# Second weight buffers and an earlier place for the ternary work in the first feed-forward layer of an adaLN transformer block

## The reference

```python
h = _layernorm(x, axis=-1) * (1 + ca) + sa
x = x + ga * _L0_attn_ref(h, wq, wk, wv, wo)
h = _layernorm(x, axis=-1) * (1 + cb) + sb
x = x + gb * _L0_ffn_ref(h, w1, w2, w3)
...
def activation_quant(x):
    scale = 127.0 / jnp.clip(jnp.max(jnp.abs(x), axis=-1, keepdims=True), EPS, None)
    return jnp.clip(jnp.round(x * scale), -128, 127) / scale
def weight_quant(w):
    scale = 1.0 / jnp.clip(jnp.mean(jnp.abs(w)), EPS, None)
    return jnp.clip(jnp.round(w * scale), -1, 1) / scale
def bitlinear(x, w):
    xn = rmsnorm(x)
    xq = xn + jax.lax.stop_gradient(activation_quant(xn) - xn)
    wq = w + jax.lax.stop_gradient(weight_quant(w) - w)
    return jnp.einsum('bsi,oi->bso', xq, wq)
h = jax.nn.silu(bitlinear(x, w1)) * bitlinear(x, w2)
return bitlinear(h, w3)
```

## Time and profile before

| what | us |
|---|---|
| median of 2 runs | 9290.5 (9260.4 to 9320.6) |
| the profiled execution | 9303.3 |
| its span on core 3, the slowest | 9301.7 |
| spans of the 8 cores | 9230.1 to 9301.7 |
| TensorE matmuls busy | 3531.4 (38%) |
| VectorE busy | 3765.0 (40%) |
| ScalarE busy | 1250.3 (13%) |
| GpSimd busy | 51.4 (1%) |

### The profile page before, as it was taken

How to read it: one execution, slowest core, us unless ns; L and a number is a source line. 1 busy time by engine, 2 the same in 40 slices (tenths; PEclk the granted TensorE clock), 3 DMA queues, 4 the chain that set the end, 5 groups by cost and what they waited for, 6 DMA issues and landing times.

```text
span 9301.7 us, 51813 instructions; the slowest of 8 cores (9230.1 to 9301.7 us)
## 1 busy us (share of the span) xinstructions
PE 3531.4 (38%) x12512; PEld 1341.4 (14%) x12512; DVE 3765.0 (40%) x5792; ACT 1250.3 (13%) x1963; POOL 51.4 (1%) x100
## 2 busy tenths in 40 slices
PE   2436666666744002344434434321111111115555
PEld 0112222222311001111111111110000000002111
DVE  3241122222213784222222222247777777762222
ACT  0135555353311000000000000000000000000000
POOL 0000000000000000000000000000000000000000
PEclk8666667677766556677677677665555555558777
DMA  9615555353033000111111111110000000014433
GB/s 156 112 27 149 154 158 145 107 150 78 19 89 77 23 0 31 61 61 52 61 61 52 61 61 52 61 41 24 24 24 24 24 27 24 24 43 121 121 120 122
DMA packets 391015, 655.95 MB, mean 71 GB/s; under 512 B 44547, under 2 KB 192006, under 8 KB 386560
## 3 DMA queue, kind: packets, MB, share of 16 engines
q1 hardware_dynamic: 376896, 560.35, 19.6%
q0 software_dynamic: 13824, 92.28, 5.8%
HBM read 693.97 MB, written 50.51 MB: 80 GB/s over the span
## 4 chain that ended last, share of the span: by engine, by line
DVE 37%; PE 23%; DMA 17%; issue 10%; ACT 6%; SPq 5%; DVEq 1%; ACTq 0%; POOLq 0%
DMA wfl<-w 11%; DVE sm L1282 8%; PE ps L1125 6%; DVE tmpb L1279 5%; PE ps L1136 5%; PE ps L1346 3%; PE ps L613 3%; DMA mring<-wmod 2%; DVE sm L1068 2%; PE ps L640 2%; PE ps L850 2%; DVE ternB L1120 2%; DVE ternA L1114 2%; ACT esb L753 1%; DVEq L74 1%
## 5 line engine op out<-in xcount | busy, mean ns | idle before, releaser
L1346 PE MATMUL ps<-q3c,ternA 128*128 128x512 bf16 x2048 | 729.9, 528 | 2354.3 <-DVE ternA L1324 2353.9
L1125 PE MATMUL ps<-q,ternA 128*128 128x512 bf16 x2048 | 572.3, 449 | 1563.5 <-DVE ternB L1120 1563.5
L1282 DVE TENSOR_TENSOR sm<-sm,tmpb 128x512 f32<-128x512 f32 x1024 | 708.8, 692 | 109.9 <-DVE tmpb L1279 4.1
L1346 PEld LDWEIGHTS ps<-q3c,ternA 128*128 128x128 bf16 x2048 | 242.0, 124 | 2842.2 <-issue 2775.1
L1149 DVE TENSOR_TENSOR rbc<-ps,du1b 128x512 f32<-128x512 f32 x128 | 88.5, 692 | 1061.0 <-PE ps L1136 1054.0
L1125 PEld LDWEIGHTS ps<-q,ternA 128*128 128x128 bf16 x2048 | 223.8, 112 | 1912.9 <-issue 1754.5
L1279 DVE TENSOR_SCALAR tmpb<-sm 128x512 f32<-128x512 f32 x1024 | 437.5, 427 | 111.0 <-DVE sm L1282 2.7
L1136 PE MATMUL ps<-q,ternB 128*128 128x512 bf16 x2048 | 452.5, 379 | 0.0
L1318 DVE TENSOR_SCALAR terntmp<-wfl,wsc 128x512 f32<-128x512 f32 x256 | 124.5, 486 | 802.6 <-DMA wfl<-w 802.5
L1363 ACT ACTIVATE kraw<-ps,modv 128x512 f32<-128x512 f32 x32 | 22.0, 687 | 3053.0 <-PE ps L1346 2965.7
L742 PE MATMUL ps<-qsb,ksb 128*128 128x512 bf16 x512 | 274.8, 549 | 335.6 <-ACT esb L753 249.9
(11 more groups left out here) (201 smaller groups left out, 4129.8 us busy)
## 6 DMA issues: line engine op xcount, KB each, us to landing
wfl<-w SPq DMA_DIRECT2D x1024, 256.0 KB, 4.4
rbc<-w SPq DMA_DIRECT2D x256, 256.0 KB, 3.9
wfl<-w SPq DMA_DIRECT2D x512, 128.0 KB, 2.3
mring<-wmod POOLq DMA_DIRECT2D x24, 2048.0 KB, 18.0
q3c<-q3s SPq DMA_DIRECT2D x384, 128.0 KB, 2.2
xst<-x2s SPq DMA_DIRECT2D x32, 512.0 KB, 3.7
hs<-hch SPq DMA_DIRECT2D x128, 128.0 KB, 1.7
hch<-hs SPq DMA_DIRECT2D x128, 128.0 KB, 2.2
```

Of the source, the lines that this page charges most:

```text
L1125: st("tensor", lambda e, th=th, kc=kc: e.matmul((psA if th == 0 else psB)[:, 0:512], ternA[:, kc * 128:(kc + 1) * 128], q12[:, kc * OWN + ...
L1282: st("vector", lambda e, tb=tb, bb=bb: e.tensor_tensor(out=tb, in0=tb, in1=bb, op=ALU.subtract))
L1346: tsl=tsl: e.matmul(psx[:, 0:512], tsl[:, di * 128:(di + 1) * 128], qsl[:, th * 512:(th + 1) * 512], start=(k3 == 0), stop=(k3 == NFC - 1)),
```

## The change

The loop body's loads and ternary work become two functions, `f1_loads` and `f1_tern`. Both are called for chunk 0 ahead of the loop, and in turn `dc2` for chunk `dc2 + 1`, ahead of the matmuls and the evacuation of chunk `dc2`. Odd chunks get buffers of their own: `wfl3` and `wfl4` for the weights, `ternA2` and `ternB2` for their ternary form. The first of the four ternary instructions now waits for the matmuls two chunks back instead of one. The first product of odd chunks goes to psE and psF, and its first matmul waits for L1149's successor of two chunks back (`w_hv[("udq", ...)]`). psC and psD, `terntmp`, `hch`, `rbc`, `sm2` and `sqb2` stay single or as they were.

```diff
--- before.py
+++ after.py
@@ -150,6 +150,10 @@
     cq3b = K.sb("cq3b", [128, 1024], F32, KB(89))
     do3b = K.sb("do3b", [128, 1024], F32, KB(93))
     terntmp = K.sb("terntmp", [128, 2048], F32, KB(97))
+    ternA2 = K.sb("ternA2", [128, 2048], BF16, KB(143))
+    ternB2 = K.sb("ternB2", [128, 2048], BF16, KB(147))
+    wfl3 = K.sb("wfl3", [128, 2048], F32, KB(159))
+    wfl4 = K.sb("wfl4", [128, 2048], F32, KB(167))
     ternA = K.sb("ternA", [128, 2048], BF16, KB(105))
     ternB = K.sb("ternB", [128, 2048], BF16, KB(109))
     hch = K.sb("hch", [128, 2048], BF16, KB(113))
@@ -1088,10 +1092,10 @@
     w_hv = {}
     w_maxi3 = st("vector", lambda e: e.memset(maxac[:, :], 0.0),
                  waits=[(sVE, w_q12)] + ([(sDBG5, 32)] if "d_cqb" in DBG else []))
-    for dc2 in range(NFC):
+    def f1_loads(dc2):
         sW = sW0 if dc2 % 2 == 0 else sW1
-        w_dst1 = wfl if dc2 % 2 == 0 else wfl2
-        w_dst2 = wfl2 if dc2 % 2 == 0 else wfl
+        w_dst1 = wfl if dc2 % 2 == 0 else wfl3
+        w_dst2 = wfl2 if dc2 % 2 == 0 else wfl4
         for cc in range(4):
             st("sync", lambda e, dc2=dc2, cc=cc, w_dst1=w_dst1: e.dma_start(
                 out=w_dst1[:, cc * 512:(cc + 1) * 512],
@@ -1102,47 +1106,64 @@
                 out=w_dst2[:, cc * 512:(cc + 1) * 512],
                 in_=w2_d[dc2][:, 4 * cc:4 * cc + 4, :]),
                inc=sW, inck=16)
-        w_wld = sW.n
-        wslc1 = wfl if dc2 % 2 == 0 else wfl2
-        wslc2 = wfl2 if dc2 % 2 == 0 else wfl
+        return sW.n
+
+    def f1_tern(dc2, w_wld):
+        sW = sW0 if dc2 % 2 == 0 else sW1
+        wslc1 = wfl if dc2 % 2 == 0 else wfl3
+        wslc2 = wfl2 if dc2 % 2 == 0 else wfl4
+        tA = ternA if dc2 % 2 == 0 else ternA2
+        tB = ternB if dc2 % 2 == 0 else ternB2
         st("vector", lambda e, wslc1=wslc1: e.tensor_scalar(
             out=terntmp[:, :], in0=wslc1[:, :], scalar1=wsc[:, 0:1], scalar2=-1.0,
             op0=ALU.is_ge, op1=ALU.add),
            waits=[(sW, w_wld), (sVE, w_negt)] +
-                 ([(sMM, w_f1mm.get(dc2 - 1, 0))] if dc2 >= 1 else
+                 ([(sMM, w_f1mm.get(dc2 - 2, 0))] if dc2 >= 2 else
                   [(sDBG2, sDBG2.n)]))
-        st("vector", lambda e, wslc1=wslc1: e.scalar_tensor_tensor(
-            out=ternA[:, :], in0=wslc1[:, :], scalar=wsc[:, 6:7], in1=terntmp[:, :],
+        st("vector", lambda e, wslc1=wslc1, tA=tA: e.scalar_tensor_tensor(
+            out=tA[:, :], in0=wslc1[:, :], scalar=wsc[:, 6:7], in1=terntmp[:, :],
             op0=ALU.is_gt, op1=ALU.add))
         st("vector", lambda e, wslc2=wslc2: e.tensor_scalar(
             out=terntmp[:, :], in0=wslc2[:, :], scalar1=wsc[:, 1:2], scalar2=-1.0,
             op0=ALU.is_ge, op1=ALU.add))
-        w_tern[dc2] = st("vector", lambda e, wslc2=wslc2: e.scalar_tensor_tensor(
-            out=ternB[:, :], in0=wslc2[:, :], scalar=wsc[:, 7:8], in1=terntmp[:, :],
+        w_tern[dc2] = st("vector", lambda e, wslc2=wslc2, tB=tB: e.scalar_tensor_tensor(
+            out=tB[:, :], in0=wslc2[:, :], scalar=wsc[:, 7:8], in1=terntmp[:, :],
             op0=ALU.is_gt, op1=ALU.add))
+
+    w_ld = {0: f1_loads(0)}
+    f1_tern(0, w_ld[0])
+    for dc2 in range(NFC):
+        if dc2 + 1 < NFC:
+            w_ld[dc2 + 1] = f1_loads(dc2 + 1)
+            f1_tern(dc2 + 1, w_ld[dc2 + 1])
+        tA = ternA if dc2 % 2 == 0 else ternA2
+        tB = ternB if dc2 % 2 == 0 else ternB2
+        psU0 = psA if dc2 % 2 == 0 else psE
+        psU1 = psB if dc2 % 2 == 0 else psF
         for th in range(2):
             for kc in range(NKC):
-                st("tensor", lambda e, th=th, kc=kc: e.matmul(
-                    (psA if th == 0 else psB)[:, 0:512],
-                    ternA[:, kc * 128:(kc + 1) * 128],
-                    q12[:, kc * OWN + th * 512: kc * OWN + (th + 1) * 512],
-                    start=(kc == 0), stop=(kc == NKC - 1)),
+                st("tensor", lambda e, th=th, kc=kc, tA=tA, psU0=psU0, psU1=psU1:
+                   e.matmul(
+                       (psU0 if th == 0 else psU1)[:, 0:512],
+                       tA[:, kc * 128:(kc + 1) * 128],
+                       q12[:, kc * OWN + th * 512: kc * OWN + (th + 1) * 512],
+                       start=(kc == 0), stop=(kc == NKC - 1)),
                    waits=([(sVE, w_tern[dc2]), (sVE, w_q12)] +
-                          ([(sVE, w_hv.get((dc2 - 1, th), 0))])
+                          ([(sVE, w_hv.get(("udq", dc2 - 2, th), 0))])
                           if kc == 0 else []),
                    inc=(sMM if kc == NKC - 1 else None))
         for th in range(2):
             for kc in range(NKC):
-                st("tensor", lambda e, th=th, kc=kc: e.matmul(
+                st("tensor", lambda e, th=th, kc=kc, tB=tB: e.matmul(
                     (psC if th == 0 else psD)[:, 0:512],
-                    ternB[:, kc * 128:(kc + 1) * 128],
+                    tB[:, kc * 128:(kc + 1) * 128],
                     q12[:, kc * OWN + th * 512: kc * OWN + (th + 1) * 512],
                     start=(kc == 0), stop=(kc == NKC - 1)),
                    waits=([(sVE, w_hv.get((dc2 - 1, th), 0))] if kc == 0 else []),
                    inc=(sMM if kc == NKC - 1 else None))
         w_f1mm[dc2] = sMM.n
         for th in range(2):
-            psu = psA if th == 0 else psB
+            psu = psU0 if th == 0 else psU1
             pst2 = psC if th == 0 else psD
             hsl = hch[:, ((2 * dc2 + th) % 4) * 512:(((2 * dc2 + th) % 4) + 1) * 512]
             sHSp = sHS[(2 * dc2 + th) % 4]
@@ -1152,6 +1173,7 @@
                waits=[(sMM, w_f1mm[dc2])] +
                      ([(sHSp, sHSp.n)] if dc2 >= 2 else []))
             w_udq = sVE.n
+            w_hv[("udq", dc2, th)] = w_udq
             st("scalar", lambda e, th=th: e.activation(
                 out=sm2[:, th * 512:(th + 1) * 512], in_=rbc[:, th * 512:(th + 1) * 512],
                 func=AF.Silu), waits=[(sVE, w_udq)])
```

## The result

The changed kernel takes 8294.5 us (median of 11 runs, 8251.9 to 8345.5) against 9277.1 us before (median of 10 runs, 9260.4 to 9331.9): 0.893 of the time, 95% interval 0.890 to 0.896. The prediction was 8285 us, range 8235 to 8430. The profiled execution took 8321.8 us.

A forecast was written before the change was run, and what follows sets the result against it. Load, ternary work, matmuls and evacuation in the first feed-forward layer stood in line, 41.07 us a turn; overlapped, 24.9 us. Over 63 turns that saves 1019 us from 9303.3, forecasting 8285 us, range 8235 to 8430.

The forecast's parts named there:

- The ring before: First feed-forward layer: load, ternary work, matmuls and evacuation follow one another without overlap, 40.95 us against 41.07 measured a turn.
- VectorE's branch: First feed-forward layer, before evacuation: load 10.38, ternary work 7.59, next instruction 0.10, together 18.07 us.
- TensorE's branch: Beside VectorE's work: last sum-of-squares matmul 1.62, about 0.1, then 16.10 us of matmuls, together 17.8 us before evacuation.
- The 0.3 us for the later of two near branches: Added to the 24.58 us turn because the later branch varies from turn to turn, giving 24.9 us.
- The added wait ahead of the evacuation: On VectorE's queue, evacuation stands behind instructions waiting for a load, so the load's 10.38 us stay on the path.
- E: As a moment: the second `hch` product's end. As a rival: work stays in line with matmuls, near 9300 us, chance 0.01.
- Clock: each turn starts slow as before: TensorE's pause shrinks to 8.2 us, still long enough for its clock to fall; the 16.10 us of matmuls stay.
- Rival A: Reduced clock, 0.81, on die 0 in the first feed-forward layer: turn 27.1 us, time 8423 us, chance 0.12.
- B: Rival: TensorE's clock stays at 1.2 GHz, matmuls 28.3 us, turn 36.5 us, time 9015 us, chance 0.04.
- C: Rival: loads land later, meeting other cores' loads; at 2 us more, turn 26.6 us, time 8391 us, chance 0.08.
- D: Rival: slower, late loads block VectorE's queue; with a 30 us load, turn 44.2 us, time 9500 us, chance 0.01.
- The sum: First feed-forward layer: 63 turns save 16.17 us each, 1019 us, other stages unchanged; 8285 us.

The follow-up runs named there:

- e1: The changed kernel with the next chunk's ternary work put back behind the evacuation, its load still early: 8802.1 us, 0.944 of before.
- e6: The changed kernel with one VectorE instruction of the ternary work doubled: 8458.9 us, 0.908 of before.
- e4: The changed kernel with the sum-of-squares matmuls behind the next chunk's first 32 matmuls, plus a second sqb buffer: 8319.9 us, 0.891 of before.
- e3: The changed kernel with loads issued two chunks ahead, same buffers: 8217.9 us, 0.881 of before.
- e5: The changed kernel with both loads two chunks ahead and sum-of-squares matmuls behind the next chunk's first 32: 7757.5 us, 0.832 of before.
- e2: The changed kernel without the second PSUM pair, all chunks using psA and psB: 8303.6 us, 0.891 of before.
- e7: The changed kernel itself run again, nothing altered: 8324.3 us (median of two), 0.894 of before.
- e8: The changed kernel with loads two chunks ahead, run once more: 8227.6 us (profiled execution) and 8256.9 us, 0.885 of before.

## Why the prediction was right, point by point

- **The ring before, 40.95 of 41.07 us.** It held: with one piece taken off, the turn fell by that piece (e1), and with one instruction added it grew by it (e6).
- **VectorE's branch, 10.38 + 7.59 + 0.10 = 18.07 us.** That it sets the turn is shown (e4, e6), its size was a little short. The ternary work kept its 7.59 us. The load took 10.22 us in the turn above, but over the 62 loads of core 0 it is 8.79 + 1.75 = 10.54 us, 0.16 more than in the sum and 0.35 more than on core 0 before. So the 0 taken for loads that overlap with matmuls was too low by that. Whether the matmuls beside them or the more frequent loads of all cores make them longer, no run separates. On core 0, whose clock never shows 0.81 in this stage, the turn is 24.89 us, where 24.9 was chosen.
- **TensorE's branch, 17.8 us.** Within half a microsecond: e3, in which it alone decides, shows 17.4. So it stands further behind VectorE's branch than the quarter of a microsecond of the prediction.
- **The 0.3 us for the later of two near branches.** Right in size (24.89 against 24.58), by luck: of the 0.31 us, waiting for late matmuls is 4.7/62 = 0.08. Half of it, 0.16, is the longer load.
- **The added wait ahead of the evacuation.** The load stayed on the path (545.3 us of L1117's idle time). SP reaches it 0.49 us after E, behind the spill, in both kernels; e3 and e5 leave it there but give it one turn more to land, and the wait is gone (6.8 us). A load put ahead of the spill, or on another queue, was not tried.
- **The second PSUM pair at nothing.** Shown by e2. The second buffers for weights and ternary form were also put at nothing beyond what they allow; no run takes them out.
- **Clock: each turn starts slow as before.** Right: L1146's mean is 451 ns on core 0, 449 before on core 3. The mean clock of the stage is 0.83 on core 0, inside the 0.8 to 0.9 of the prediction's signs, but 0.76 on core 2.
- **Rival A.** It took part, and its price was right: where the stage ran at 0.81 on the slowest core, turns took 27.1 us, exactly the rival's figure. As this was 574 us of the stage, the mean turn was 26.02 us, about halfway between 24.9 and 27.1. 63 x (26.02 - 24.89) = 71 us, which is the distance of core 2 from core 0 in the profile (what they differ by ahead of and behind the stage, 16 and 17 us, cancels). The condition was wrong in part. In the stretch of the earlier trace rows the clock is 0.79 and 0.81 on cores 2 and 3 but 0.97 on cores 0 and 1, so there too it was not all of die 0. And a denser stage alone does not bring it: in e5's profile TensorE is busy 90% of the stage and no core leaves 1.00 after the first burst, and e3 puts the same matmuls into turns of 23.9 us without 0.81. For e5 this rests on one profile; two other executions of it have mean clocks of 0.677 to 0.682 on some cores against 0.69 on the others, in which stage is not known.
- **B, C, D and E** did not come: on the six cores without 0.81 matmuls reach full clock in each turn, and nothing fell in line again. Of C a small part came: the mean load is 10.5 to 10.8 us on the cores of the two profiles of this kernel, against 10.38 in the sum, where C put 2 us more.
- **The sum.** Core 2 went from 9283.0 to 8320.2 us, 963 less. Its turn before was (6150.61 - 3569.08)/63 = 40.98 us, so 63 x (40.98 - 26.02) = 942 of them lie in the stage. The rest lies where the code is unchanged: the stage began 34 us earlier (at 3535.34), and what follows it took 13 us more. The medians differ by 983 us, where 1019 were forecast. The 36 us between lie between what 0.81 cost the slowest core in the profile (71 us) and in e7 (63 x (25.37 - 25.04) = 21 us); that it is the cause in the median is not shown. The time itself came within 10 us of the forecast partly by luck: 8285 was counted from the profiled execution's 9303.3 us, 26 us above the median of 9277.1. From that median the same saving gives 8258 us.

## What to carry to other kernels

Where a loop has two branches of like length between one meeting point and the next, shortening either gives almost nothing (here 1.0 and 0 us of 25), and shortening both gives the whole (8.8 us); before judging an edit that "did nothing", look at who waits now. A queue that is worked through in order decides what prefetching is worth: the load was moved a full chunk ahead in the code, but it still stood behind the spill on SP and so began at the same point of the turn, 0.49 us after E. Work out the waits of each queue from the point at which all branches meet, and add them branch by branch.

## What the runs showed of the hardware that was not expected

- In the first feed-forward layer the granted clock of 0.81 came to pairs of cores (2 and 3 in the changed kernel, 2 and 3 and 6 and 7 in e7, 0 and 1 in e2), never to a whole die, and not where TensorE was busiest: it was absent in e5's stage (busy 90%) and present in the changed kernel's (busy about 70%). It was absent in the profiles of e1, e3, e4, e6 and e8 as well. The Trainium skill (TensorE: Matmul & The Clock Gate, "Seeing it yourself") says that a whole die goes to 13/16 of its clock once three of its cores run dense matmuls; in this stage the level agrees with the 0.81 seen, the whole die and the dense matmuls do not. Elsewhere both pictures occur: from 2260 to 2500 us of e4, in the projections and attention, the four cores of die 0 show 0.79 to 0.81 and those of die 1 0.93 to 0.96, while e6 and e8 have no 0.81 on any core in the whole profile. What brings it on stays open; no run here was made to find it.
- In e5, the pause between bursts of matmuls is about 1.5 us (of L1141's 605.9 us of idle time about 510 are the wait before the first chunk, the rest is spread over 63 turns), and after the first burst the clock did not fall to 1.2 GHz in the stage: L1141's mean is 380 ns. With the pause of some 8 us in e3 it is 442 ns; that is (561.0 - 455.2)/64 = 1.7 us a turn.
